# Two fill-in steps per key block, and halved matmul pieces, in a transformer layer on eight cores

## What is computed

```python
qkv = layernorm(x) @ Wqkv + bqkv              # q, k, v: heads of 64
attn = softmax(causal(q @ k.T / 8)) @ v       # per head
x = x + attn @ Wproj + bproj
h = layernorm(x)
y = x + (h @ W.T + b) + (h @ V_r) @ C.T       # V_r, C: rank 32
```

## Time and profile before

| | us |
|---|---|
| device time, two runs | 897.61 and 952.88 (median 925.24) |
| device time of the profiled execution | 896.85 |
| its span (slowest core, core 4) | 895.3 |
| spans of the eight cores | 884.1 to 895.3 |
| busy in the span: TensorE | 701.6 (78%) |
| busy: ScalarE | 352.8 (39%) |
| busy: VectorE | 281.2 (31%) |
| busy: GpSimd | 186.2 (21%) |
| mean granted TensorE clock of the eight cores | 0.866 to 0.888 |

### The profile page before, as it was taken

The page is one execution under the profiler, slowest core; times in us unless marked ns, Lnnn a source line. Parts: engine busy times, 40 slices in busy tenths (PEclk is TensorE's granted clock), DMA queues, the critical chain, the costliest instruction groups (busy, mean ns, idle before and its releaser), DMA issues.

```text
span 895.3 us, 11459 instructions; the slowest of 8 cores (884.1 to 895.3 us)
## 1 busy us (share of the span) xinstructions
PE 701.6 (78%) x3433; PEld 297.5 (33%) x3433; DVE 281.2 (31%) x675; ACT 352.8 (39%) x769; POOL 186.2 (21%) x304
## 2 busy tenths in 40 slices
PE   0499999997168888888888897889897878666756
PEld 0244444443033333333333333333232323222322
DVE  2443434202025422344232334311232232433242
ACT  0141414130025554644655657575757576300000
POOL 2000000001025333332222324221212222320401
PEclk9999999999555557789889999989899999878687
DMA  8990200001930000011010100101010000111001
GB/s 162 215 201 20 77 18 23 1 1 20 165 97 1 1 1 25 1 47 48 1 48 1 48 24 25 48 1 48 1 35 14 25 25 1 47 48 47 24 24 47
DMA packets 15131, 38.18 MB, mean 43 GB/s; under 512 B 3401, under 2 KB 3425, under 8 KB 15073
## 3 DMA queue, kind: packets, MB, share of 16 engines
q0 software_dynamic: 7616, 11.67, 8.7%
q1 hardware_dynamic: 7457, 25.79, 8.1%
HBM read 39.68 MB, written 8.39 MB: 54 GB/s over the span
## 4 chain that ended last, share of the span: by engine, by line
PE 70%; DVE 9%; ACT 7%; issue 6%; DMA 4%; POOL 2%; DVEq 0%; SPq 0%; ACTq 0%; POOLq 0%
PE ps_pv L412 15%; PE ps_sp L428 9%; PE ps_w L543 7%; PE ps_sp L255 6%; PE ps_pv L255 6%; PE ps_u L428 4%; PE ps_w L612 4%; ACT xnt_a L435 4%; PE ps_pv L612 4%; PE ps_bf L239 4%; PE ps_sp L282 3%; PE ps_w L282 3%; ACT xf_a L435 3%; DMA xf_a<-wffn 3%; PE ps_w L591 1%
## 5 line engine op out<-in xcount | busy, mean ns | idle before, releaser
L435 ACT ACTIVATE xnt_a<-ps_sp 128x512 bf16<-128x512 f32 (+3 forms) x285 | 141.6, 538 | 146.0 <-PE ps_sp L428 112.4
L428 PE MATMUL ps_sp<-q_fm,k_fm 64*128 64x512 bf16 (+3 forms) x427 | 134.3, 392 | 44.4 <-ACT xnt_a L435 28.9
L442 POOL TENSOR_TENSOR xnt_a<-xnt_a,tri_sb 128x128 bf16<-128x128 bf16 x142 | 57.6, 427 | 257.8 <-ACT xnt_a L435 256.9
L412 PE MATMUL ps_pv<-xnt_a,v_on 128*66 128x512 bf16 (+3 forms) x356 | 109.7, 412 | 1.7 <-POOL xnt_a L442 1.4
L428 PE MATMUL ps_u<-q_fm,k_fm 64*128 64x512 bf16 (+2 forms) x213 | 83.3, 391 | 23.7 <-ACT xf_a L435 14.9
L435 ACT ACTIVATE xf_a<-ps_u 128x512 bf16<-128x512 f32 (+3 forms) x142 | 76.1, 536 | 51.7 <-PE ps_sp L428 44.1
L412 PE MATMUL ps_pv<-xf_a,v_on 128*66 128x512 bf16 (+3 forms) x284 | 88.2, 404 | 2.5 <-POOL xf_a L442 1.7
L435 ACT ACTIVATE xf_a<-ps_sp 128x512 bf16<-128x512 f32 (+3 forms) x142 | 70.9, 541 | 48.1 <-PE ps_sp L428 26.5
L442 POOL TENSOR_TENSOR xf_a<-xf_a,tri_sb 128x128 bf16<-128x128 bf16 x114 | 46.4, 427 | 142.7 <-ACT xf_a L435 141.4
L428 PEld LDWEIGHTS ps_sp<-q_fm,k_fm 64*128 64x128 bf16 x427 | 33.1, 95 | 127.6 <-issue 123.1
L481 DVE RECIPROCAL recips<-ps_bf 128x4 f32<-128x4 bf16 x64 | 11.7, 183 | 185.7 <-PE ps_bf L471 182.4
(11 more groups left out here) (73 smaller groups left out, 770.2 us busy)
## 6 DMA issues: line engine op xcount, KB each, us to landing
xf_a<-x SPq DMA_DIRECT2D x32, 512.0 KB, 3.4
y<-xf_a SPq DMA_DIRECT2D x16, 512.0 KB, 2.7
wq_a<-wqkv POOLq DMA_DIRECT2D x3, 2048.0 KB, 39.6
wq_a<-wproj POOLq DMA_DIRECT2D x1, 2048.0 KB, 19.7
xf_a<-wffn POOLq DMA_DIRECT2D x4, 512.0 KB, 26.2
bias_a<-bqkv POOLq DMA_DIRECT2D x1, 512.0 KB, 55.6
bias_a<-bffn POOLq DMA_DIRECT2D x1, 512.0 KB, 59.5
bias_a<-bproj SPq DMA_DIRECT2D x1, 512.0 KB, 9.2
```

The source lines that it names most:

```text
L412: e.matmul(ps_pv[hd][0:66, off * 128:512], v_on[:, ki2, 66 * hh:66 * hh + 66], chunk(cb)[:, 0:ncol], start=st, stop=sp),
L428: e.matmul(sbanks[sb][:, off * 128:512], k_fm[hp:hp + 64, hc, ki * 128:(ki + 1) * 128], q_fm[hp:hp + 64, hc, g * 512 + off * 128:(g + 1) * ...
L435: e.activation(chunk(cb)[:, 0:ncol], sbanks[sb][:, off * 128:512], AF.Exp, bias=0.0, scale=0.125),
L442: gate = P.op("pool", lambda e, cb=cb: e.tensor_tensor(chunk(cb)[:, 0:128], chunk(cb)[:, 0:128], tri01[:], ALU.mult), waits=[m_ex, m_cm], ...
```

## The change

`pump()` is called twice per iteration in place of once. The projection and the FFN get a further yield in the middle of each column half, behind the fourth of its eight matmuls. "c" has 9 yields in place of 7, "a2" 5 in place of 3. No operation, wait, buffer or transfer is added or taken away; only the order of the engines' lists changes, in blocks 1 to 3 of the attention.

```diff
--- before.py
+++ after.py
@@ -448,6 +448,7 @@
                 if ki % 2 == 1:
                     pop_pv()
                 pump()
+                pump()
             pop_pv(drain=True)
             if defer is not None:
                 defer[1]()
@@ -546,6 +547,8 @@
                                         start=(kc == 0), stop=(kc == KC - 1)),
                                waits=[m_aoT, m_wproj, r_psw] if (half == 0 and kc == 0) else [],
                                sig="pe" if (half == 1 and kc == KC - 1) else None)
+                    if kc == 3:
+                        yield
                 yield
             r_aoT[i2] = mmp
             m_x2 = P.op("dve", lambda e, i2=i2, i3=i3: e.scalar_tensor_tensor(
```

## The result

The change makes the kernel 7.5% slower: 965.6 us (median of 11 runs) against 897.3 (10 runs), ratio 1.075 with a 95% interval of 1.072 to 1.078. The forecast was 920, or 2.5%, with a range up to 932. The sign was right; the loss is three times the forecast one. The profiled execution has a span of 955.8 us against 895.3, 60.5 more.

The account below looks back on a forecast made before the run. In blocks 1 to 3 neither TensorE nor ScalarE is full, so the order of TensorE's list decides. 19.0 us for blocks 2 and 3, 1.0 for block 1 and 2.8 for clock, on 896.85, gave 920 us, range 902 to 932.

Parts of the forecast that it names:

- heavy pairs: Attention pairs with generators "c" and "a2"; forecast 2.9 us longer each, or 2.2 with a half-clock fall at the start.
- light pairs: Attention pairs with generators "b" and "a1"; their transposes move from iteration 4 to 2, forecast to cost nothing.
- Layout of a heavy pair: Second pair of block 2: stand-stills of 0.7, 1.0 and 1.6 us and later light iterations cost 2.9 us, bounds 2.1 to 3.3.
- Half clock in some pairs: Six of eight heavy pairs, blocks 2 and 3: a half-clock fall at the start covers 0.7 us, leaving 2.2 each.
- Light pairs: nothing: Light pairs: transposes two iterations earlier still meet the division's end, with five or six scores issued; cost nothing.
- Block 1: Block 1: two heavy pairs cost 5.2 us, the vanishing ScalarE wait gives 4.2 back; 1.0 net, bounds -4 to +5.
- More half clock: Rival, chance 0.13: one more fall to half clock in each of ten heavy pairs, 34 us more, 931 us.
- Packing holds the clock up: Rival, chance 0.12: denser full-array work in blocks 1 to 3 removes half-clock time, 28 us saved, 889 us.
- Backlog worked off: Rival, chance 0.25: iterations 7 and 8 of heavy pairs run without bank waits, costing 2.1 or 1.4 us each; 910 us.
- The signs: Attention waits: projection's from 3.0 to about 16 us, new ones before transposes and narrow matmuls, ScalarE's 4.2 towards 0.

Follow-up runs that it names:

- e6: Changed kernel with idle matmuls in all four TensorE stand-stills and four more yields putting light pairs' transposes back in iteration 4: 925.4 us, ratio 1.034.
- e3: Changed kernel with one more yield behind the store of y, so scores and products stand ahead of the projection again: 954.1 us, ratio 1.064.
- e12: Kernel before the change without the yield behind the second FFN half, so the projection stands right behind the last correction: 925.4 us, ratio 1.031.
- e7: Kernel before the change with only the light pairs' transposes moved two iterations earlier, to iteration 2: 925.3 us, ratio 1.033.
- e5: Changed kernel with four more yields ahead of the light pairs' transposes, which puts them back in iteration 4: 948.4 us, ratio 1.060.
- e4: Changed kernel, order kept, with idle matmuls or transposes filling all four TensorE stand-stills, results overwritten unread: 951.7 us, ratio 1.060.

## Why the prediction was wrong

The growth of the span by groups of pairs (core 4 before, core 1 after; a pair runs from the row of line 471 or 472 at the end of the one before it to its own):

| | before | after | more | at half clock |
|---|---|---|---|---|
| 8 heavy pairs, blocks 2 and 3 | 198.7 | 240.4 | 41.7 | 21 to 56 us |
| 7 light pairs, blocks 2 and 3 | 137.5 | 144.7 | 7.2 | 24 to 44 us |
| block 1 and pair 0 of block 2 | 132.7 | 146.4 | 13.7 | 59 to 82 us |
| all before and behind | 426.4 | 424.3 | -2.1 | |

In e6, with the gaps filled and the light transposes late, these three are 221.0, 139.9 and 136.9 us on its slowest core. The eight heavy pairs at full clock throughout would have been 4 x 21.4 + 4 x 26.4 = 191.2 before. So of the 62.6 us in the first three rows, 221.0 - 191.2 = 29.8 are the packing of those pairs at equal clock, about 4 are its share in block 1 (an estimate: pairs 5 to 7 of block 1 and pair 0 of block 2 of e6 against the kernel before), and the other 29 are clock: 12 in the heavy pairs (240.4 - 221.0, less 198.7 - 191.2), 7 in the light ones, 10 in block 1.

By the prediction's own steps:
- **Layout of a heavy pair: right, a little short.** The waits were forecast at 0.7, 1.0 and 1.6 us and are 0.7, 0.7 and 1.55 on average, the ScalarE wait went, and the order was as laid out. One wait was missed: the first FFN quarter goes into the bank of `ps_w` from which the small copy of line 598 reads, and waits for it, 0.53 us ten times. The cost at full clock was put at 2.9 us, at most 3.3, and is 3.7 (the earlier trace rows against the windows of e6); with the missed wait the layout gives 3.4.
- **"Half clock in some pairs": failed.** I let dips cover part of the gaps, 0.7 us in each of six pairs, and put two more dips on top, 2.8 us. The changed heavy pairs have more dips, and the covering did not show: in block 3 a heavy pair takes 31.4 us with one dip and 33.0 with two, against 27.6 with one before. Forecast for all clock effects: 2.8 - 4.2 = -1.4 us; measured: +29. This is the largest error. Which gap brings the dips stays open. Filling all four takes them away (e6: no half clock in a heavy pair of blocks 2 and 3, on any core). Closing the longest alone doesn't (e3: 68 us on the slowest core), and that one alone in the kernel before doesn't bring them (e12: 22 us against 21).
- **"Light pairs: nothing": failed.** I asked whether the earlier transposes would have to wait, found they would not, and stopped. They were also the only full-array work in some 20 us, and with early ones a dip in the pair can last to its end and beyond. Moving them alone costs 30 us (e7); moving them back in the changed kernel gives 13 (e5).
- **Block 1: put at 1, measured 13.7.** The wait of 4.2 us did go, but both heavy pairs there are 5 to 8 us longer, pair 6 is 2.5 shorter, and pair 0 of block 2 fell to half clock for most of its length on the slowest core (21.9 us, against 17.5 on cores where it did not).
- **The rivals.** "More half clock", at 931 us with 0.13, was about right for the heavy pairs: a dip more in each. The eight of blocks 2 and 3 have 35 us more at half clock, for 12 us. It had nothing for light pairs and block 1. "Packing holds the clock up" did not come: the clock of all three stretches fell. In "Backlog worked off" nothing came true.
- **The signs.** The waits ahead of the transposes, the narrow matmuls and the projection came, and the ScalarE wait went, as said. One sign of being wrong came too: the clock of the three stretches moved by 0.05, 0.05 and 0.08, where over 0.03 was to count against the forecast. Pair 7 of block 3 takes 32.7 us at a lower clock, not 29.3 at 1.00.

The rule of the Trainium skill (TensorE: Matmul & The Clock Gate, "HAM oscillation — how this bites in real kernels") says that bursts broken by waits fall back to half clock; its example has waits for DMA. e4 agrees for the waits together: with the gaps filled, half-clock time in the heavy pairs of its slowest core is 17 us in place of 56. e3 and e12 don't bear it out for the longest wait alone. I had weighed the rule against one heavy pair without a dip and let that count too much.

## What to carry to other kernels

When fill-in work is moved among low-utilisation matmuls, note for each stretch where its full-array matmuls stand and what the granted clock does behind them, on all cores; a move that adds next to no wait can still cost several per cent. Count the distance between every VectorE step and the matmul that needs it in instructions of the queue, bank reuse included: two steps per iteration halve it even though each piece is smaller. And where TensorE sits at half clock with idle time to spare, test whether cheap idle matmuls pay; in blocks 0 and 1 they gave 12 us.

## What the hardware showed

- A stretch of scores and products with v runs at either clock from end to end. The same light pair of block 3 takes 20.5 us at full clock and 29.1 at half. In the runs with early transposes the long stretches at half clock last 10 to 38 us; some end behind transposes or FFN matmuls, some at the start of the next pair, ahead of any.
- Adding matmuls made kernels faster, twice: ratio 1.075 to 1.060 for filled gaps, and 0.996 to 0.982 for idle work in blocks 0 and 1.
- Over the eight cores a pair of blocks 2 and 3 with the same time at half clock has the same length, to 0.4 us in the kernel before and 0.3 in the changed one, so pair length against time at half clock separates what a change costs in waits from what it costs in clock, within one execution.
